# Local attention in a two-block transformer: the Newton step of the reciprocal norms on VectorE in place of GpSimd

## What is computed

```python
def l2norm(t):
    return t / jnp.maximum(jnp.linalg.norm(t, axis=-1, keepdims=True), 1e-12)

def attn_layer(x, Wqkv, qs, ksc, Wo):                  # 16 heads of 64
    q, k, v = jnp.split(x @ Wqkv, 3, -1)
    q = l2norm(q) * qs
    k = l2norm(k) * ksc
    q = q * cos * scale + rotate_half(q) * sin * scale
    k = k * cos * inv + rotate_half(k) * sin * inv
    return local_attention(q, k, v) @ Wo               # window 32, softmax(8 * q k)

for i in range(6):
    x = attn_layer(shift_tokens(x), ...) + x
    x = ffn_layer(shift_tokens(x), ...) + x
```

## Time and profile before

| | us |
|---|---|
| median of 3 runs | 4636.0 |
| lowest and highest | 4634.15 and 4636.34 |
| the profiled execution | 4636.16 |
| its span in the profile | 4634.3 |
| VectorE busy (share of the span) | 3486.1 (75%) |
| GpSimd busy | 2803.0 (60%) |
| ScalarE busy | 2548.2 (55%) |
| TensorE busy | 4220.5 (91%) |

### The profile page before, as it was taken

One profiled execution on the slowest core, in us unless ns is written; L12 is line 12 of the kernel. 1 busy time (PEld: TensorE's weight loads), 2 busy tenths in 40 slices (PEclk: granted clock), 3 DMA queues, 4 the chain that ended last, 5 costly groups with the idle time before them and its releaser, 6 DMA issues.

```text
span 4634.3 us, 148124 instructions
## 1 busy us (share of the span) xinstructions
PE 4220.5 (91%) x51751; PEld 2916.6 (63%) x51751; DVE 3486.1 (75%) x7330; ACT 2548.2 (55%) x5842; POOL 2803.0 (60%) x3446
## 2 busy tenths in 40 slices
PE   4999996999899988999889998999889998588799
PEld 2777774666656656666656666666666666466565
DVE  3666657999589976999679985999779996566466
ACT  1555554666466654666456663666546664355322
POOL 1333336889288873898468882888648883355200
PEclk9999998999999999999999998999999999688699
DMA  2000000000100001000100001000000001000000
GB/s 80 7 7 7 7 22 11 5 5 6 41 6 4 5 25 23 5 5 7 32 14 5 5 6 42 6 4 5 29 20 5 5 6 26 20 12 12 2 7 11
DMA packets 160436, 64.06 MB, mean 14 GB/s; under 512 B 121364, under 2 KB 155936, under 8 KB 159520
## 3 DMA queue, kind: packets, MB, share of 16 engines
q1 hardware_dynamic: 160288, 62.05, 5.2%
HBM read 26.54 MB, written 2.10 MB: 6 GB/s over the span
## 4 chain that ended last, share of the span: by engine, by line
PE 35%; DVE 29%; issue 25%; ACT 4%; POOL 4%; DVEq 1%; SPq 1%; ACTq 1%; DMA 0%; POOLq 0%
DVE ss L947 6%; DVE big L942 6%; DVE mx L959 5%; PE pj L1463 4%; DVE big L941 3%; DVE e L966 3%; DVE qn L941 3%; PE pj L1306 3%; PE sc L1475 3%; PE turn L1382 3%; PE pp L1264 2%; ACT big L655 2%; PE turn L1463 2%; PE po L1279 2%; PE sc L1622 1%
## 5 line engine op out<-in xcount | busy, mean ns | idle before, releaser
L1364 PE MATMUL pj<-wqkv,xcT 128*128 128x512 f32 x1536 | 830.8, 624 | 23.9 <-DVE big L942 9.0
L647 ACT ACTIVATE big<-pj 128x512 f32<-128x512 f32 x768 | 459.1, 598 | 243.8 <-PE pj L1364 175.8
L506 POOL TENSOR_TENSOR big<-big 128x512 f32<-128x512 f32 x384 | 486.2, 1277 | 142.2 <-DVE big L942 142.2
L942 DVE TENSOR_TENSOR big<-pj,ropes 128x512 f32<-128x512 f32 x768 | 522.1, 680 | 0.0
L506 POOL TENSOR_TENSOR qn<-qn,big 128x512 f32<-128x512 f32 x384 | 486.4, 1276 | 35.0 <-DVE big L942 35.0
L947 DVE TENSOR_REDUCE ss<-big 128x8 f32<-128x512 f32 x768 | 503.9, 677 | 0.2 <-ACT big L647 0.2
L1452 PEld LDWEIGHTS pp<-wo,oT 128*128 128x128 f32 x3072 | 366.9, 196 | 154.5 <-ACT oT L670 154.1
L501 POOL TENSOR_TENSOR e<-e,rc 128x512 f32<-128x512 f32 x384 | 392.9, 1045 | 47.4 <-DVE rc L977 47.4
L1452 PE MATMUL pp<-wo,oT 128*128 128x128 f32 x3072 | 404.0, 286 | 7.0 <-ACT oT L670 7.0
L495 POOL TENSOR_TENSOR qn<-qn,ny 128x512 f32<-128x512 f32 x384 | 397.1, 1046 | 7.5
L495 POOL TENSOR_TENSOR big<-big,ny 128x512 f32<-128x512 f32 x384 | 396.6, 1045 | 7.5
(11 more groups left out here) (298 smaller groups left out, 9587.1 us busy)
## 6 DMA issues: line engine op xcount, KB each, us to landing
wqkv<-in_L_ffn_Wqkv SPq DMA_DIRECT2D x6, 1536.0 KB, 6.4
xsd<-Y SPq DMA_DIRECT2D x192, 32.0 KB
xsd<-Y SPq DMA_DIRECT2D x384, 15.8 KB
xsf<-Y SPq DMA_DIRECT2D x96, 64.0 KB
xsf<-Y SPq DMA_DIRECT2D x192, 31.5 KB
xsx<-Y SPq DMA_DIRECT2D x64, 64.0 KB, 1.8
xsx<-CT SPq DMA_DIRECT2D x64, 64.0 KB, 1.9
wo<-in_L_ffn_Wo SPq DMA_DIRECT2D x6, 512.0 KB, 7.4
```

The costliest lines, as they stand in the source:

```text
L506: nc.gpsimd.tensor_tensor(U[a.par][i], U[a.par][i], t2b[i % 2], ALU.add).then_inc(sem("d_add"), 1)
L647: nc.scalar.activation(sqb[i % 2], pj[i % 2][:, :], ACT.Square).then_inc(sem("d_sq"), 1)
L942: nc.vector.tensor_tensor(t2v, swapped, sin, ALU.mult).then_inc(sem("d_r"), 1)
L1364: mm(pj[i % 2][:, :], xcT[:, a.par, :], wqkv[:, i * 512:i * 512 + 512], start=True, stop=True).then_inc(sem("d_ch"), 1)
```

## The change

The Newton step moves from GpSimd to VectorE, where it stands as `polish` between row_max(0) and below_max(0). It takes three operations: w = ny ssc, w = w ny, ny = (w - 3) ny. That leaves out the factor -0.5, which goes into the rope tables instead. GpSimd's unit(a, 0) waits for the third operation; the clamp no longer waits for the old Newton step.

```diff
--- before.py
+++ after.py
@@ -457,7 +457,7 @@
             nc.gpsimd.memset(l_half[:, 0:2], 0.5)
             nc.gpsimd.memset(l_half[:, 2:4], 0.5 / S)
             nc.gpsimd.memset(l_la[:, :], 0.0).then_inc(sem("l_la0"), 1)
-            head_start(pool, "l_ga", "l_os", "l_km", "l_xb", "l_z", "x_p", "d_un", "d_pr", "d_add", "d_nt", "f_eps", "f_rstd")
+            head_start(pool, "l_ga", "l_os", "l_km", "l_xb", "l_z", "x_p", "d_un", "d_pr", "d_add", "f_eps", "f_rstd")
             nc.gpsimd.memset(xsd[:, :, :], 0.0)
             nc.gpsimd.memset(xsf[:, :, :, :], 0.0).then_inc(sem("edge"), 1)
             pool.wait_ge(sem("edge"), 1)
@@ -489,7 +489,7 @@
                 def unit(tile, i):
                     if tile:
                         if i == 0:
-                            past(pool, "d_nt", tile.g * 4 + 4)
+                            past(pool, "d_nt", tile.g * 3 + 3)
                         past(pool, "d_add", tile.g * 4 + (i + 1))
                         uv = U[tile.par][i].rearrange("p (h d) -> p h d", d=DK)
                         nc.gpsimd.tensor_tensor(uv, uv, bc(ny[:, tile.par, 8 * i:8 * i + 8], DK), ALU.mult).then_inc(sem("d_un"), 1)
@@ -513,17 +513,6 @@
                 turn_sum(0)
                 turn_sum(1)
                 turn_sum(2)
-                if a:
-                    y, w = ny[:, a.par, :], nw[:, :]
-                    past(pool, "d_rn", a.g + 1)
-                    nc.gpsimd.tensor_tensor(w, y, y, ALU.mult).then_inc(sem("d_nt"), 1)
-                    past(pool, "d_nt", a.g * 4 + 1)
-                    nc.gpsimd.tensor_tensor(w, w, ssc[:, :], ALU.mult).then_inc(sem("d_nt"), 1)
-                    past(pool, "d_nt", a.g * 4 + 2)
-                    past_waits(pool, "went_on")
-                    nc.gpsimd.tensor_scalar(w, w, -0.5, 1.5, ALU.mult, ALU.add).then_inc(sem("d_nt"), 1)
-                    past(pool, "d_nt", a.g * 4 + 3)
-                    nc.gpsimd.tensor_tensor(y, y, w, ALU.mult).then_inc(sem("d_nt"), 1)
                 unit(a, 0)
                 turn_sum(3)
 
@@ -844,7 +833,7 @@
                 dve.wait_ge(sem("y_ready" if n == 2 else "n_t"), NT * (n if n == 1 else 1 if n == 2 else n - 1))
                 nc.vector.tensor_copy(tmp[:, 0:1], mean[:, 0:1]).then_inc(sem("n_y"), 1)
 
-            head_start(dve, "l_gs", "l_c1", "l_rc1", "l_t1", "l_t2", "l_mx1", "l_mx2", "l_sb1", "l_sb2", "l_res", "x_ev", "x_m", "x_r", "x_c1", "x_res", "d_r", "d_ss", "d_cl", "d_mx", "d_sub", "d_sm", "d_rc", "d_res",
+            head_start(dve, "l_gs", "l_c1", "l_rc1", "l_t1", "l_t2", "l_mx1", "l_mx2", "l_sb1", "l_sb2", "l_res", "x_ev", "x_m", "x_r", "x_c1", "x_res", "d_r", "d_ss", "d_cl", "d_nt", "d_mx", "d_sub", "d_sm", "d_rc", "d_res",
                        "f_xn", "f_hT", "f_st", "f_ag", "f_mv")
             dve.wait_ge(s_ld, NLOAD)
             nc.vector.tensor_scalar(law[:, 1:2], law[:, 0:1], -1.0, 1.0, ALU.mult, ALU.add)
@@ -949,7 +938,6 @@
                 def clamp():
                     if a:
                         past(dve, "d_ss", a.g * 4 + 4)
-                        past(dve, "d_nt", a.g * 4)
                         nc.vector.tensor_tensor(ssc[:, :], ss[:, :, :].rearrange("p c h -> p (c h)"), tiny[:, :], ALU.max).then_inc(sem("d_cl"), 1)
 
                 def row_max(p):
@@ -975,6 +963,17 @@
                         past(dve, "d_sm", b.g * 2 + (p + 1))
                         past(dve, "d_pr", b.g * 2 + (p - 1))
                         nc.vector.reciprocal(rc[:, p, 0:8], sm[:, p, 0:8]).then_inc(sem("d_rc"), 1)
+
+                def polish():
+
+                    if a:
+                        y, w = ny[:, a.par, :], nw[:, :]
+                        past(dve, "d_rn", a.g + 1)
+                        nc.vector.tensor_tensor(w, y, ssc[:, :], ALU.mult).then_inc(sem("d_nt"), 1)
+                        past(dve, "d_nt", a.g * 3 + 1)
+                        nc.vector.tensor_tensor(w, w, y, ALU.mult).then_inc(sem("d_nt"), 1)
+                        past(dve, "d_nt", a.g * 3 + 2)
+                        nc.vector.scalar_tensor_tensor(y, w, 3.0, y, ALU.subtract, ALU.mult).then_inc(sem("d_nt"), 1)
 
                 rope(0)
                 square_sum(0)
@@ -986,6 +985,7 @@
                 clamp()
                 rope(3)
                 row_max(0)
+                polish()
                 below_max(0)
                 row_max(1)
                 below_max(1)
@@ -1042,7 +1042,7 @@
                 dve.wait_ge(sem("att_loaded"), l * ATT_LOADS + ATT_LOADS)
                 past(dve, "d_r", l * (NT * 4))
                 for w, (cn, sn) in enumerate((("qcos", "qsin"), ("kcos", "ksin"))):
-                    temper = 1.0 if w else QK_SCALE
+                    temper = -0.5 if w else -0.5 * QK_SCALE
                     nc.vector.scalar_tensor_tensor(rc_[:, w, :], const(cn), temper, qs[:, w, :], ALU.mult, ALU.mult)
                     nc.vector.scalar_tensor_tensor(rs_[:, w, 0:32], const(sn)[:, 0:32], temper, qs[:, w, 32:64], ALU.mult, ALU.mult)
                     last = nc.vector.scalar_tensor_tensor(rs_[:, w, 32:64], const(sn)[:, 32:64], temper, qs[:, w, 0:32], ALU.mult, ALU.mult)
```

## The result

The changed kernel takes **4715.5 us** (median of 4 runs, 4705.6 to 4723.6) against 4636.2 (4 runs, 4634.2 to 4637.4) of the kernel before on the same chip: **1.0167 times as long, 95% interval 1.0154 to 1.018**. The forecast was 4695 with 4664 to 4755.

A forecast was written before the change was run, and what follows sets the result against it. The prediction took two loops, through the softmax and through GpSimd, to bound the kernel. The longer costs 0.45 - 0.13 = 0.32 us a tile, 186 times 59.5 us, on 4636: 4695 us, range 4664 to 4755.

The forecast's parts named there:

- What bounds the kernel: Steady tile of 13.41 us: two loops matter, through the softmax and through GpSimd, with 0.13 and 0.12 us of slack.
- loop A: From row_max(0) on VectorE through ScalarE's exponentials and TensorE's chunk(1) to the next tile's rope(1); 0.13 us of slack.
- loop B: GpSimd's unit(a,0) to the next turn_sum(0), which frees rope(2)'s buffer, then VectorE to row_max(0); 0.12 us of slack.
- The three operations: On VectorE between row_max(0) and below_max(0): starts 0.25 us apart, below_max(0) 0.45 us later.
- The price of a tile: Steady tile: the 0.45 us delay less 0.13 of slack makes it 0.32 us longer.
- Fill and drain: Start and end of each layer: gain or lose some tenths of a us, left out of the forecast.
- The sum: Whole kernel: 186 tiles at 0.32 us each add 59.5 us to 4636, giving 4695 us.
- The new wait of GpSimd: Ahead of unit(a,0): GpSimd idles about 2.5 us for VectorE's third operation, starting 0.42 later, 0.30 a tile after slack.
- The rest covers it: VectorE's 0.84 us rest ahead of rope(0) absorbs the delay, no change, 4636 us; chance 0.05.
- The clamp comes free: VectorE's clamp goes ahead of GpSimd's turn_sum(2): 45 us faster, 4591; chance 0.05 together with the other faster rival.
- The read path is contested: GpSimd's SBUF reads hold each new VectorE operation like the clamp: 1.77 us a tile, 4965 us; chance 0.03.
- GpSimd's relief: 1.39 us leave GpSimd's queue, so unit(a,0) starts earlier and loop B shortens; chance 0.05 together with the other faster rival.

The follow-up runs named there:

- polish_first: Changed kernel with the three VectorE operations ahead of row_max(0) in place of behind it: 4723.0 us, 1.0188 times the kernel before.
- half_wo_before: Kernel before with half of the output projection's matmuls left out (4 of 8 a tile): 4634.0 us, 0.9988 times the kernel before.
- after_pad1: Changed kernel with one idle semaphore instruction more on VectorE behind below_max(1) in each step: 4691.8 us in one run; timed again, 4697.1.
- no_clamp_after: Changed kernel without the clamp, ScalarE adding 1e-24 in its Ln: 4633.3 us, 0.9988 times the kernel before.
- no_clamp_before: Kernel before without the clamp, ScalarE adding 1e-24 in its Ln, Newton step still on GpSimd: 4628.4 us, 0.998 times the kernel before.
- clamp_const_before: Kernel before with the clamp against a constant in place of a tile of constants: 4636.5 us, 0.9997 times the kernel before.
- no_newton: Kernel before with the Newton step left out on either engine, units waiting for ScalarE's ny: 4632.8 us, 0.999 times the kernel before.

## Why the prediction came out as it did

- **What bounds the kernel:** incomplete, without harm to the number. Loops A and B exist and their slack was read against the tile as it was, 13.41; what set that was loop C, which the text doesn't name. Its rows could have been read beforehand: TensorE's back-to-back stretch from chunk(2) to chunk(0).
- **The three operations:** right. 0.18 to 0.19 long, starts 0.21 to 0.22 apart where I took 0.25; the handoff to below_max(0) took 0.03 after the last one's end where I took 0.04 of overlap. The two errors cancel, which is luck: 0.45 forecast, 0.45 measured.
- **The price of a tile:** right in every first tile, 0.45 - 0.13 = 0.32 (13.73). Mis-sized in every second, 0.54 - 0.13 = 0.41 (13.82). "186 x 0.32 = 59.5" should read 93 x 0.32 + 93 x 0.41 = 67.9; the profile shows 67.0. That loop B costs 0.32 where 0.30 was forecast is luck too: its delay was 0.36 and not 0.42, its slack 0.04 and not 0.12.
- **Fill and drain:** "some tenths of a us and is left out" is the step that failed. In the profiled execution the five stretches between layers cost 10.5 us. The delay alone is some tenths, as forecast: behind the first layer's last clamp, with the clock at 1.00, the last tile's row_max comes 14.29 us behind the clamp, where before it was 13.94 behind every layer with the clock at 1.00 (all but the first). What the forecast left out is TensorE's clock. In the 16 us behind the third layer's last clamp it averages 0.79 of its full 2.4 GHz, so a good part ran at the 1.2 GHz level, where before it was 1.00 throughout (the second row of the windows above). The changed kernel, behind the first and the third layer:

```profile
1174.09:1190.09 16.00, 12.94 (x260) 9.94 (x258) 8.27 (x18) 8.19 (x17) 7.99 (x8) 1.00 0.01 2
...
2272.70:2288.70 16.00, 13.27 (x224) 9.84 (x226) 6.68 (x15) 8.11 (x16) 8.00 (x8) 0.79 0.01 2
```

  As many us of TensorE time hold fewer matmuls, 224 for 260, and the third layer's row_max comes 16.55 us behind the clamp. Over the five stretches the clock stood at its lower level for 150.2 us, before for 129.7; 20.5 us more at half the clock are an estimated 10.2 us if TensorE set the pace in all of them. Why the clock fell sooner was not tried, and a longer tile alone doesn't do it: in polish_first, whose tile is longer still, it stays at 1.00 in these 16 us behind three of the six layers, and in half_wo_before, whose tile is 0.03 shorter and whose TensorE has less to do, behind none. The loss isn't the same in each execution: the same five stretches cost 3.1 us more than before in after_pad1. The runs of the changed kernel lie 18 us apart, those of the kernel before 3.
- **The sum:** 67 + 10.5 = 77.5 of the 79.3 between the medians. That it comes so near is partly luck, since both parts are from the longest of four executions; the shortest is 69.5 us over the kernel before, hardly more than the tiles' 67. The remaining 10 of the profiled execution lie ahead of the first clamp and behind the last. 2.6 of them are the last layer's own drain (row_max 16.52 behind the clamp in place of 13.94); in the rest the change does nothing. Behind the last clamp the clock stood at its lower level for 300.0 us, before for 283.0.
- **The new wait of GpSimd:** right, 2.5 us forecast and 2.48 measured; GpSimd's busy time fell by 183.4 us where 184 was forecast. That loop B stays behind loop A holds for the second tile of a pair; in the first the two are level.
- **The rivals.** *The rest covers it:* fell; VectorE's rest ahead of rope(0) only went from 0.84 to 0.64. *The clamp comes free:* it did not. no_clamp_after shows what it is worth to the changed kernel: all of the loss in a tile, but not the 45 us under the kernel before, since loop C stands at 13.41; no_clamp_before brings 0.2% for the same reason. *The read path is contested:* fell, 0.18 to 0.19. The rule that explains the clamp (the Trainium skill, SBUF — State Buffer, section Who interferes with whom) also counts VectorE's tensor_scalar, with its one SBUF input, as a possible contender, since it can enter a mode that takes the ports shared with GpSimd; clamp_const_before agrees with 0.761 us. *GpSimd's relief:* fell twice: polish_first hands the norms over sooner and takes 4723.0, and no_newton removes the step and gains 0.1%. VectorE is faster at it (0.19 against 0.25 us), and the kernel slower.

The fastest version of those run that computes the whole result is no_clamp_before, 4628.4 us, 0.2% under the kernel before.

## What to carry to other kernels

Before a small step is moved to another engine, write down every loop that the tile closes, with the slack of each against the tile's time; a step that is hidden on its old engine saves nothing there, and on the new one it costs its length and its handoffs less the slack, whatever the engine's speed. When shortening one loop brings nothing, look for the one standing beside it: two cuts that bring 0.1 to 0.2% alone can bring 3% together. Check a change also where the pipeline runs empty: here the end of a layer came 0.35 us later with TensorE's clock at 1.00 and 2.6 us later with it at 0.79.

## What was not expected of the hardware

- The 0.09 us ahead of one operation in every second step, which one idle instruction elsewhere in VectorE's program removes (93 of them are 8.4 us over the kernel).
- A VectorE operation of 128x32 with one SBUF input and a constant waits for GpSimd's running operation as one with two inputs does: 0.761 us against 0.18 undisturbed.
- TensorE's granted clock fell to an average of 0.79 in the drain of a layer whose tiles were only 0.32 and 0.41 us longer, while behind the first layer of the same execution it stayed at 1.00.
